# Attention output projection as three split passes, and every other copy of the keys on ScalarE

## What is computed

```python
def _layer(x, wqkv, qs, ksc, wo, lg, lb, w1, b1, w2, b2):
    h = shift_token(x)
    q, k, v = jnp.split(h @ wqkv, 3, axis=-1)
    ...
    q = l2norm(q) * qs
    k = l2norm(k) * ksc
    q, k = rotary_xpos(q, k)
    o = local_attention(q, k, v)
    o = o.transpose(0, 2, 1, 3).reshape(b, n, INNER)
    x = x + o @ wo
    ...
```

## Time and profile before

| | |
|---|---|
| three executions | 1762.49, 1766.63, 1765.33 us; median 1765.33 |
| the profiled execution | 1770.82 us, its span 1769.0 us |
| TensorE, busy share of the span | 95% |
| VectorE | 76% |
| ScalarE | 74% |
| GpSimd | 63% |
| TensorE's mean granted clock | 0.989 of full speed |

### The profile page before, as it was taken

One profiled execution on the slowest core, in us unless ns is written; L12 is line 12 of the kernel. 1 busy time (PEld: TensorE's weight loads), 2 busy tenths in 40 slices (PEclk: granted clock), 3 DMA queues, 4 the chain that ended last, 5 costly groups with the idle time before them and its releaser, 6 DMA issues. The chain is left out here.

```text
span 1769.0 us, 43496 instructions
## 1 busy us (share of the span) xinstructions
PE 1683.6 (95%) x15560; PEld 1093.5 (62%) x15560; DVE 1341.4 (76%) x2369; ACT 1307.5 (74%) x4472; POOL 1121.7 (63%) x1012
## 2 busy tenths in 40 slices
PE   8998899999989999998999999899999989999999
PEld 5664677775657777554344444577776557777655
DVE  5555898984778989456788887889885688898654
ACT  5445788887358888745899999788887538888863
POOL 5555899992579999603212221799995278999730
PEclk9999999999999999999899999999999999999999
DMA  3001111103011110202655552211102102110111
GB/s 90 2 2 42 25 32 26 26 20 87 13 39 27 28 28 18 70 1 38 130 92 101 97 96 46 60 26 31 26 20 55 51 1 55 26 32 20 43 31 42
DMA packets 67310, 74.90 MB, mean 42 GB/s; under 512 B 13381, under 2 KB 50969, under 8 KB 65049
## 3 DMA queue, kind: packets, MB, share of 16 engines
q1 hardware_dynamic: 67096, 72.13, 19.2%
HBM read 28.08 MB, written 10.49 MB: 22 GB/s over the span
## 5 line engine op out<-in xcount | busy, mean ns | idle before, releaser
L536 POOL TENSOR_TENSOR rsum<-pa,pb 128x512 f32<-128x512 f32 x256 | 325.6, 1293 | 65.4 <-DVE pa L452 35.2
L908 ACT ACTIVATE ffn_prob<-sc,ffn_nmax 128x128 f32<-128x128 f32 x928 | 327.6, 387 | 4.8 <-DVE ffn_nmax L824 4.8
L993 POOL TENSOR_TENSOR ffn_prob<-ffn_prob,ffn_rden 128x512 f32<-128x512 f32 x256 | 265.6, 1059 | 52.2 <-DVE ffn_rden L839 44.6
L545 POOL TENSOR_TENSOR rsum<-rsum,ffn_rnt 128x512 f32<-128x512 f32 x256 | 261.9, 1045 | 10.8 <-ACT ffn_rnt L930 8.5
L462 DVE TENSOR_TENSOR pb<-proj,tab 128x512 f32<-128x512 f32 x236 | 161.8, 686 | 89.0 <-ACT rn L506 88.5
L908 ACT ACTIVATION_READ_ACCUMULATOR ffn_prob<-sc,ffn_nmax 128x1 f32 x928 | 210.4, 227 | 0.0
L442 PE MATMUL pt<-ident,rsum 128*128 128x128 f32 x960 | 154.0, 283 | 10.0 <-POOL rsum L545 7.3
L824 DVE TENSOR_REDUCE ffn_nmax<-sc 128x4 f32<-128x512 f32 x232 | 148.6, 682 | 12.9 <-PE sc L723 10.0
L442 PEld LDWEIGHTS pt<-ident,rsum 128*128 128x128 f32 x960 | 100.7, 140 | 91.2 <-ACT ffn_ptb L916 70.5
L473 DVE TENSOR_REDUCE ffn_ss<-rn 128x16 f32<-128x1024 f32 x128 | 154.6, 1208 | 0.0
L452 DVE TENSOR_TENSOR pa<-proj,tab 128x512 f32<-128x512 f32 x236 | 150.8, 680 | 0.0
(11 more groups left out here) (322 smaller groups left out, 4318.1 us busy)
## 6 DMA issues: line engine op xcount, KB each, us to landing
ffn_v<-ffn_v SPq DMA_DIRECT2D x128, 128.0 KB, 2.3
column_ks<-qk_parts SPq DMA_DIRECT2D x64, 128.0 KB, 4.1
rn<-Y SPq DMA_DIRECT2D x32, 128.0 KB, 2.3
qk_parts<-column_hi SPq DMA_DIRECT2D x64, 64.0 KB, 1.6
qk_parts<-column_lo SPq DMA_DIRECT2D x64, 64.0 KB, 1.6
column_qs<-qk_parts SPq DMA_DIRECT2D x32, 128.0 KB
column_qs<-qk_parts SPq DMA_DIRECT2D x64, 64.0 KB
rn<-Y SPq DMA_DIRECT2D x32, 127.5 KB, 2.4
```

Of the source, the lines that this page charges most:

```text
L536: pool.tensor_tensor(K.sm[:, r, w], K.m1[:, r, w], K.m2[:, r, w], ALU.add).then_inc(S.f_sum, 1)
L545: pool.tensor_tensor(heads(K.sm[:, r, w]), heads(K.sm[:, r, w]), K.rnt[:, r, w * HEADS:(w + 1) * HEADS].unsqueeze(2).broadcast_to([P, HEAD ...
L908: ins = act.activation(K.prob[:, r, e, k], score_banks(i)[e][:, tokens(k)], ACT.Exp, bias=K.nmax[:, r, e, k:k + 1], accum_out=K.den[:, r, ...
L993: pool.tensor_tensor(K.prob[:, r, e], K.prob[:, r, e], K.rden[:, r, e].unsqueeze(2).broadcast_to([P, 4, P]), ALU.mult).then_inc(S.f_pn, 1)
```

## The change

The output projection of the attention becomes a split product: `wo` is loaded to a staging place and GpSimd makes its high and low part (`split_output_weights`). The output's copy out of `ob` now goes to a float32r tile `ghi` of two buffers (semaphore `f_oh`), and VectorE takes the low part `ob` - `ghi` into `glo` (`keep_low`). `f_ot`, which frees `ob` and starts the projection, is now given by `keep_low`. The keys of tiles with an odd number are copied by ScalarE, just ahead of its copy of the queries, in place of VectorE; in the MLP stage's part of a layer VectorE still copies all.

```diff
+def split_output_weights(pool, K, n):
+    pool.wait_ge(S.wa_wo, 16 * (n + 1))
+    pool.tensor_copy(K.wo_hi[:], output_stage(K)).then_inc(S.wo_hi, 1)
+    pool.wait_ge(S.wo_hi, n + 1)
+    pool.tensor_tensor(K.wo_lo[:], output_stage(K), K.wo_hi[:].bitcast(F32), ALU.subtract).then_inc(S.wo_lo, 1)
...
+            if m == 4:
+                pe.wait_ge(S.wo_lo, n + 1)
             if i >= 2:
                 pe.wait_ge(S.f_ot, TILES * n + i - 1)
...
-            if i == 0:
-                pe.wait_ge(S.wa_wo, 16 * (n + 1))
-            pe.matmul(K.ss[:], K.wo[:, c], K.ot[:, c], start=(c == 0), stop=(c == CHUNKS - 1)).then_inc(S.f_wo, 1)
+            pe.matmul(K.ss[:], K.wo_hi[:, c], K.ghi[:, i % 2], start=(c == 0), stop=False)
+            pe.matmul(K.ss[:], K.wo_lo[:, c], K.ghi[:, i % 2], start=False, stop=False)
+            pe.matmul(K.ss[:], K.wo_hi[:, c], K.glo[:, i % 2], start=False, stop=(c == CHUNKS - 1)).then_inc(S.f_wo, 1)
...
         def keep_output(i):
             dve.wait_ge(S.f_pv, TILES * n + i + 1)
-            dve.wait_ge(S.f_wo, TILES * n + i - 3)
-            dve.tensor_copy(K.ot[:, i % 4], K.ob[:]).then_inc(S.f_ot, 1)
+            dve.wait_ge(S.f_wo, TILES * n + i - 1)
+            dve.tensor_copy(K.ghi[:, i % 2], K.ob[:]).then_inc(S.f_oh, 1)
+        def keep_low(i):
+            dve.wait_ge(S.f_oh, TILES * n + i + 1)
+            dve.tensor_tensor(K.glo[:, i % 2], K.ob[:], K.ghi[:, i % 2].bitcast(F32), ALU.subtract).then_inc(S.f_ot, 1)
...
+            if LATE + 1 < i < TILES:
+                keep_low(i - 2)
             if i == TILES - 1:
                 keep_output(i - 1)
+                keep_low(i - 1)
             if i == TILES:
                 gate_normal(dve, K, n, 0)
                 keep_output(i - 1)
+                keep_low(i - 1)
...
-            if 0 <= j - 1 < TILES - 1:
-                keep_keys(dve, K, n, j - 1, pt[1])
+            if 0 <= j - 1 < TILES - 1 and j % 2:
+                keep_keys(dve, dve.tensor_copy, K, n, j - 1, pt[1])
             if i == LATE:
                 maxima(i + 1)
+            if 1 <= i <= LATE:
+                keep_low(i - 1)
...
         def keep_output(i):
             act.wait_ge(S.f_pv, TILES * n + i + 1)
-            if i >= 4:
-                act.wait_ge(S.f_wo, TILES * n + i - 3)
-            act.copy(K.ot[:, i % 4], K.ob[:]).then_inc(S.f_ot, 1)
+            if i >= 2:
+                act.wait_ge(S.f_wo, TILES * n + i - 1)
+            act.copy(K.ghi[:, i % 2], K.ob[:]).then_inc(S.f_oh, 1)
...
+            if 0 <= j - 1 < TILES - 1 and j % 2 == 0:
+                keep_keys(act, act.copy, K, n, j - 1, pt[1])
...
+            if begin < 0 and i == -2:
+                split_output_weights(pool, K, n)
...
             split_value_weights(pool, K, n + 1)
+            split_output_weights(pool, K, n + 1)
```

More of the change, by code:

```diff
@@ L249, in query_key_stage, with output_stage @@
             room[:, 3 * INNER:3 * INNER + 4 * DH].rearrange("p (b d) -> p b d", d=DH))
+def output_stage(K):
+    return K.stage[:, 6 * INNER:7 * INNER].rearrange("p (c n) -> p c n", n=P)
 def load_query_key_weights(sp, K, n):
@@ L267, in load_value_weights @@
     sp.dma_start(K.stage[:, part], d["L0_ffn_wqkv"][l, :, part]).then_inc(S.wa_w[2], 16)
-    sp.dma_start(K.wo[:], d["L0_ffn_wo"][l].rearrange("(c p) n -> p c n", p=P)).then_inc(S.wa_wo, 16)
+    sp.dma_start(output_stage(K), d["L0_ffn_wo"][l].rearrange("(c p) n -> p c n", p=P)).then_inc(S.wa_wo, 16)
 def split_query_key_weights(pool, K, n):
@@ L299, in split_value_weights @@
     pool.tensor_tensor(K.wqkv_lo[2], part, K.wqkv_hi[2].bitcast(F32), ALU.subtract).then_inc(S.wa_lo, 1)
+def split_output_weights(pool, K, n):
+    S = K.s
+    pool.wait_ge(S.wa_wo, 16 * (n + 1))
+    pool.tensor_copy(K.wo_hi[:], output_stage(K)).then_inc(S.wo_hi, 1)
+    pool.wait_ge(S.wo_hi, n + 1)
+    pool.tensor_tensor(K.wo_lo[:], output_stage(K), K.wo_hi[:].bitcast(F32), ALU.subtract).then_inc(S.wo_lo, 1)
 def load_mlp_weights(sp, K, n):
@@ L477, in norms, with keep_keys @@
     dve.tensor_reduce(K.ssc[:], K.ss16[:], AX.X, ALU.max).then_inc(S.f_cl, 1)
-def keep_keys(dve, K, n, j, bank):
+def keep_keys(engine, copy, K, n, j, bank):
     S = K.s
     q, t = divmod(j, 4)
-    dve.wait_ge(S.f_ttk, TILES * n + j + 1)
+    engine.wait_ge(S.f_ttk, TILES * n + j + 1)
     if q >= 2 and t == 0:
-        dve.wait_ge(S.f_sc, 2 * TILES * n + 8 * (q - 1))
-    dve.tensor_copy(K.kT[:, q % 2, :, tokens(t)], blocks(bank[:])).then_inc(S.f_tk, 1)
+        engine.wait_ge(S.f_sc, 2 * TILES * n + 8 * (q - 1))
+    copy(K.kT[:, q % 2, :, tokens(t)], blocks(bank[:])).then_inc(S.f_tk, 1)
 def high_parts(dve, K, n, q):
@@ L1230, in early @@
             if (x - 7) % 3 == 1 and 2 <= (x - 7) // 3 < LEAD + 1:
-                keep_keys(dve, K, n + 1, (x - 7) // 3 - 2, K.ss)
+                keep_keys(dve, dve.tensor_copy, K, n + 1, (x - 7) // 3 - 2, K.ss)
         for x in range(UPS):
@@ L2103, in __init__ @@
         self.wa_wo = new("wa_wo")
+        self.wo_hi = new("wo_hi")
+        self.wo_lo = new("wo_lo")
         self.wa_hi = new("wa_hi")
@@ L2135, in __init__ @@
         self.f_pv = new("f_pv")
+        self.f_oh = new("f_oh")
         self.f_ot = new("f_ot")
@@ L2234, in ffn @@
         K.w1_lo = sb("w1_lo", [P, 6 * P], F32R)[:, 0:2 * HID]
-        K.wo = sb("wo", [P, CHUNKS, P])
+        K.wo_hi = sb("wo_hi", [P, CHUNKS, P], F32R)
+        K.wo_lo = sb("wo_lo", [P, CHUNKS, P], F32R)
         K.w2 = sb("w2", [P, 3, P])
@@ L2250, in ffn @@
         K.ptb = sb("ptb", [P, 2, 2, 4, P])
-        K.ot = sb("ot", [P, CHUNKS, PAIR])
         K.m1, K.m2, K.sm = K.pa, K.pb, K.rsum
@@ L2263, in ffn @@
         K.nq, K.nl = (K.ptb[:, r].rearrange("p e k j -> p e (k j)") for r in range(2))
-        K.nr = K.ot[:, 0:2]
+        K.nr = sb("nr", [P, 2, PAIR])
         K.gl, K.u = (x[:, 0].rearrange("p e k j -> p e (k j)") for x in (K.prob, K.ptb))
```

## The result

| | before | after |
|---|---|---|
| median, us | 1764.86 (1762.49 to 1766.63, 4 runs) | 1798.07 (1794.54 to 1800.41, 4 runs) |
| ratio to before, 95% interval | | 1.0187 [1.0166, 1.0209] |
| profiled execution, us | 1770.82 (span 1769.0) | 1797.37 (span 1795.2) |

The change costs 33 us. The forecast was 1793.0, between 1775 and 1810, and slower.

A forecast was written before the change was run, and what follows sets the result against it. TensorE, busy 95% of the span, was taken as the bound, with the other three engines close to full. Terms -1 + 14.4 + 12 + 2.6 = 28 us on the 1765.33 median gave 1793 us, range 1775 to 1810.

The forecast's parts named there:

- No gain from the passes: Projection: shorter split passes gain almost nothing, as the next transposes wait for ScalarE's copy out of `pt[1]`; -1 us.
- The stall of 0.6 us at i = 4, 8, ..., 24: Steady loop: where values come first, TensorE waits for VectorE's subtraction; 24 x 0.6 = 14.4 us.
- The keys' copies at nothing: Odd i: keys' copy on ScalarE delays its queries' copy and squares by 0.48 us, but this is covered; no cost.
- VectorE falls behind by about 0.5 us and makes it good one i later: Keys' copies, one kind of odd i: VectorE's delay is absorbed where it had idled over 1 us.
- The end of a layer: From i = 28 each subtraction stands on the chain, hidden again from i = 32; +3.0 us a layer, 12 us for four.
- an i other than each fourth stalls: Sign of being wrong: in the loop only i = 4, 8, ..., 24 should stall.
- The weights' split: GpSimd's added cast and subtraction delay a scaling TensorE waits for, 1.3 us in layers 0 and 2; 2.6 us.
- passes count in full: Rival: transposes wait for the projection, not ScalarE, so all 0.14 us counts, 18 us; 1776 us; chance 0.08.
- contended subtraction: Rival: float32r output or GpSimd's reads stretch the subtraction to 0.93 us; 1810 us; chance 0.12.
- shorter stalls: Rival: layer ends partly absorbed or steady stall 0.4 us; 1784 us; counted with the forecast, together 0.66.
- cancelled: Rival: gain and stalls both at half, time within 0.2% of no change; chance 0.05.
- faster: Rival: ScalarE's chain moves ahead by the stall, 14.4 us vanish and ends cost half; -9, 1756 us; chance 0.09.

The follow-up runs named there:

- one pass: Changed kernel without the low part of the output, and with only the first of the three projection passes; 1771.26 us, ratio 1.0028.
- the mended end: Changed kernel with subtractions moved ahead of other VectorE work, and ScalarE's output rounding between exponential halves, at each layer's end; 1780.02 us, ratio 1.0103.
- the last kernel: Changed kernel, full result: layer ends reordered, halves swapped up to i=24, weights split three steps earlier, early rounding and subtraction at i=3, 7, ..., 23; 1764.20 us, ratio 1.0002.
- swapped halves: Changed kernel with the two halves of the probabilities transposed and normalised in the other order, `pt[1]` first; 1794.83 us, ratio 1.0165.
- the load without the wait: Changed kernel with the subtraction replaced by an equally long VectorE reduction that the projection waits for and the values don't; 1783.75 us, ratio 1.0090.

## Why the prediction was right, point by point

- **No gain from the passes** (-1 us): right in the steady tiles, and for the reason given. The time of one pass against three is the proof. The gain that there is lies at the ends of the layers, where the prediction counted none: 0.76 us a layer without the subtraction, 0.5 in the changed kernel. That the trace agrees with three quarters of a projection was said too firmly: 0.72 of 0.86 us is 0.84.
- **The stall of 0.6 us at i = 4, 8, ..., 24** (14.4): 0.59 in the drift, 24 times, 14.2. The subtraction was put at 0.68 us with no contention and took 674 to 694 ns in all 128. The Trainium skill, "SBUF — State Buffer", section "Who interferes with whom", has no contention for an instruction with one SBUF input. The trace agrees, with GpSimd busy for 110.81 of 121.01 us beside it.
- **The keys' copies at nothing**: right in the steady tiles, where the working leaned on the stall as cover. A drift of 0.08 us five times a layer, 1.6 us in all, is there with all keys on VectorE too; its cause is open. At i = 27 the copies do cost: the changed kernel loses 0.70 us there, and 0.26 with the keys back on VectorE, so 0.44, or 1.8 us in four layers. The step that failed is "VectorE falls behind by about 0.5 us and makes it good one i later": at the end of a layer it isn't made good. The working spoke of ScalarE's and VectorE's slack, and the delay passes through GpSimd.
- **The end of a layer** (3.0 each, 12 in all): step by step +1.06, +1.77, +2.72 and +3.12 were measured where +1.0, +1.8, +2.7 and +3.2 stood. The last two projections give 0.5 back, so 2.66. Not foreseen is a loss of 0.70 us at i = 27, ahead of these, with no query and key products left to issue. Two things meet there. The values wait 1.33 us for the subtraction, which stands behind the keys' copy on VectorE (395.41 above), and VectorE is late by then through the keys on ScalarE. With the subtraction moved ahead 0.48 stays, with the keys back on VectorE 0.26. The step that failed is the sentence that puts the start of the trouble at i = 28; "an i other than each fourth stalls" was one of the prediction's own signs of being wrong. Together 3.36 us, 13.4 for four.
- **The weights' split** (2.6): mis-sized. GpSimd and TensorE of the kernel after, start of layer n = 0, against the earlier trace rows:

```profile
184.16 0.61 POOL L311 CAST ffn_wo_hi<-ffn_v 128x512 fp32r<-128x512 f32 x1
184.84 1.26 POOL L313 TENSOR_TENSOR ffn_wo_lo<-ffn_v,ffn_wo_hi 128x512 fp32r<-128x512 f32 x1
186.06 2.04 POOL L559 TENSOR_TENSOR rsum<-rsum,ffn_rnt 128x512 f32<-128x512 f32 x2
190.65 2.04 POOL L559 TENSOR_TENSOR rsum<-rsum,ffn_rnt 128x512 f32<-128x512 f32 x2
...
187.25 2.09 PE L456 MATMUL pt<-ident,rsum 128*128 128x128 f32 x8 [2.65 <-POOL rsum L559]
```

  The wait grows from 1.38 to 2.65 us, the 1.3 expected. But ahead of the scaling after that one GpSimd had idled 0.59 us in the kernel before, and runs on without a gap now, so half a microsecond comes back:

```profile
190.12 2.04 POOL L545 TENSOR_TENSOR rsum<-rsum,ffn_rnt 128x512 f32<-128x512 f32 x2 [0.59 <-ACT ffn_rnt L930]
```

  From the cast of the value weights to the first projection n = 0 takes 46.79 us in place of 46.03, and n = 2 takes 45.20 in place of 44.78: 1.2 us for the two layers. In all four TensorE ran a part of the stretch at its lower clock (granted 0.94 to 0.99), which blurs the comparison. At full clock (granted 1.00) the stretch took 44.16 us in n = 2 of the kernel with the mended end, which splits the weights at this place, and 43.11 in the last kernel, which splits them three steps earlier: 1.05 a layer, 2.1 for two. So 2.6 was too much, by 0.5 to 1.4.
- **The sum**: 14.2 for the stalls, 1.6 for the small drifts, 13.4 for the ends and 1.2 to 2.1 for the split are 30 to 31 us by the traces. The times give 33 +- 4, and 30 at equal clock; 28 were predicted. Part of that closeness is luck: 2.8 us at i = 27 and 1.6 of small drifts were missing, 2 us of gain at the ends as well, and the split stood too high.

Of the rivals, "passes count in full" is excluded by the run with one pass, "contended subtraction" by the durations, "shorter stalls" by the 0.59 us of each, "cancelled" by the time, "faster" by the stalls. The condition of the last was that the subtraction must come some 0.5 us earlier. The last run made it nearly so, and ended at the kernel before's time, not below it.

## What to carry to other kernels

Ask of a shorter instruction what its successor waits for: here the view of waits showed, before any change, that the weight loads behind the projection stood 108 times at ScalarE's copy, and 0.47 us less work per tile was worth 1 us in all until that copy could start earlier. A step that is put between a buffer's last use and its release is paid where the next writer comes early, which is also where a loop runs out of other work: go through its last iterations one by one. And count an order in iterations of each engine by itself; the same edit one tile off cost 15 us.

## What was not expected of the hardware

TensorE's clock fell in some layers and not in others that did the same. Kernel with swapped halves, end of layers n = 0 and n = 2 (columns as in the first fence; the granted clock is the third number from the end):

```profile
396.79:406.79 10.00, 6.59 (x83) 4.84 (x83) 3.98 (x8) 7.64 (x36) 2.04 (x2) 1.00 0.56 131
406.79:410.79 4.00, 4.00 (x55) 3.28 (x59) 1.80 (x4) 3.39 (x17) 2.04 (x2) 0.64 0.01 4
...
1362.56:1372.56 10.00, 6.59 (x82) 4.84 (x83) 3.98 (x8) 7.64 (x36) 2.04 (x2) 1.00 0.57 132
1372.56:1376.56 4.00, 4.00 (x71) 3.28 (x71) 1.81 (x4) 3.42 (x18) 2.04 (x2) 1.00 0.02 4
```

Ahead of both TensorE was busy for 6.59 of 10 us, with no idle time longer than 1.38 us. Then it ran a part of 4 us at the lower of its two levels (1.2 in place of 2.4 GHz) in one and none in the other, and the 24 small products of the attention output took 1.81 us in place of 1.12:

```profile
407.68 1.81 PE L768 MATMUL ob<-ffn_ptb,ffn_v 128*64 128x128 f32 x24
...
1373.45 1.12 PE L768 MATMUL ob<-ffn_ptb,ffn_v 128*64 128x128 f32 x24
```

It costs 1.5 us a time: the drift from one projection to the next is 2.97 us in n = 0 and 1.38 in n = 2. It came in two of four layers with this kernel and with the load without the wait, whose end of a layer leaves TensorE similar gaps, and in none after the change. The starts of layers show the same: from the cast of the value weights to the first projection of n = 0 the kernel before took 46.03 us at a granted clock of 0.94, and with swapped halves 43.07 at 1.00. What decides which layer is hit stays open.
